# Routed token rows kept as two 16-bit planes and fetched transposed by the DMA queue

## What is computed

```python
x = layernorm(x + attention(x))          # 16 heads, 4 shared key/value heads, causal
logits = einsum('ed,btd->bte', gate_w, x)
scores = sigmoid(logits) + gate_b
weights, indices = top_k(scores, 4)      # 4 of 16 experts for each token
weights = weights / weights.sum(-1)
shared = silu(x @ w1_shared) * (x @ w3_shared) @ w2_shared
# routed expert e on a token row: silu((x @ w1[e]) * (x @ w3[e])) @ w2[e]
x = layernorm(x + shared + sum of the four routed results, weighted)
```

## Time and profile before

| | |
|---|---|
| runs, median (lowest to highest) | 598.32 us (597.01 to 599.32) |
| span of the profiled execution, first to last instruction | 564.5 us |
| median less span, what lies around the instructions | 33.8 us |
| PE / PEld busy | 527.0 / 358.6 us |
| DVE / ACT / POOL busy | 439.9 / 370.1 / 295.3 us |
| DMA packets, bytes | 53693, 64.95 MB |

### The profile page before, as it was taken

How to read it: one execution, slowest core, us unless ns; L and a number is a source line. 1 busy time by engine, 2 the same in 40 slices (tenths; PEclk the granted TensorE clock), 3 DMA queues, 4 the chain that set the end, 5 groups by cost and what they waited for, 6 DMA issues and landing times.

```text
span 564.5 us, 12179 instructions
## 1 busy us (share of the span) xinstructions
PE 527.0 (93%) x3786; PEld 358.6 (64%) x3786; DVE 439.9 (78%) x1122; ACT 370.1 (66%) x831; POOL 295.3 (52%) x340
## 2 busy tenths in 40 slices
PE   8999999999999899989999898899999999999770
PEld 4656444445454454534433487799999999999760
DVE  2387989899889799999991269988787877876582
ACT  2444767787888588869688574467676767676132
POOL 5121231656304657358888773777545454544671
PEclk9999999999999899989999999999999999999995
DMA  5954174500632902321132541586444334321962
GB/s 145 173 75 54 30 196 131 82 5 20 99 89 63 211 30 60 65 77 60 42 123 80 167 131 40 166 257 204 150 142 128 117 109 131 117 82 46 398 233 74
DMA packets 53693, 64.95 MB, mean 115 GB/s; under 512 B 8075, under 2 KB 47390, under 8 KB 53632
## 3 DMA queue, kind: packets, MB, share of 16 engines
q1 hardware_dynamic: 45952, 46.45, 32.0%
q0 software_dynamic: 7056, 17.60, 9.0%
q10 hardware_dynamic: 624, 0.13, 0.1%
HBM read 32.49 MB, written 25.62 MB: 103 GB/s over the span
## 4 chain that ended last, share of the span: by engine, by line
PE 70%; DVE 13%; POOL 6%; issue 4%; ACT 2%; DMA 2%; SPq 1%; ACTq 0%; POOLq 0%; DVEq 0%
PE psH L1678 14%; PE psS L1479 10%; PE psO L1464 9%; PE psT L1449 8%; PE psS L1541 4%; POOL xs_scratch L755 3%; DVE MX L1143 3%; PE psG L1689 3%; PE psX L1646 3%; PE psS L1484 2%; PE psY L1702 2%; PE psY L1706 2%; PE psY L1703 2%; PE psY L1704 2%; PE psY L1705 2%
## 5 line engine op out<-in xcount | busy, mean ns | idle before, releaser
L882 ACT ACTIVATE prob<-psT 128x512 f32<-128x512 f32 (+3 forms) x384 | 167.6, 496 | 54.4 <-PE psT L1449 51.9
L1143 DVE TENSOR_REDUCE MX<-psS 128x1 f32<-128x512 f32 (+3 forms) x344 | 183.2, 597 | 11.4 <-PE psS L1484 5.6
L1479 PE MATMUL psS<-KS,QS 96*128 96x512 bf16 (+3 forms) x384 | 110.9, 330 | 4.9 <-DVE MX L1143 2.5
L828 POOL DMA_INDIRECT y_scratch<-ys,dst x79 | 77.1, 976 | 65.6 <-ACT ys L1037 50.7
L1449 PE MATMUL psT<-QS,KS 98*128 98x512 bf16 (+3 forms) x384 | 107.8, 330 | 1.6 <-DMA QS<-MT 0.7
L784 POOL TENSOR_SCALAR_AFFINE_SELECT prob<-prob 128x512 f32<-128x512 f32 x64 | 42.5, 665 | 97.7 <-ACT prob L882 97.5
L1464 PE MATMUL psO<-prob,V 128*32 128x512 f32 (+3 forms) x768 | 82.8, 506 | 1.1 <-POOL prob L784 1.0
L1678 PE MATMUL psH<-wU,xh 128*128 (+1 forms) x380 | 80.7, 334 | 0.5 <-DVE z L1295 0.4
L755 POOL DMA_INDIRECT xs_scratch<-x1row,slotu x64 | 65.7, 1027 | 26.9 <-issue 16.2
L1449 PEld LDWEIGHTS psT<-QS,KS 98*128 98x128 bf16 x384 | 33.9, 98 | 54.6 <-ACT prob L882 34.2
L1479 PEld LDWEIGHTS psS<-KS,QS 96*128 96x128 bf16 x384 | 37.4, 99 | 46.0 <-DVE MX L1143 23.8
(11 more groups left out here) (252 smaller groups left out, 990.3 us busy)
## 6 DMA issues: line engine op xcount, KB each, us to landing
xs<-xs_scratch SPq DMA_DIRECT2D x80, 134.0 KB, 2.3
y<-y_scratch SPq DMA_DIRECT2D x16, 512.0 KB, 10.1
QS<-qp SPq DMA_DIRECT2D x48, 128.0 KB, 5.1
wU_raw<-in_L_ffn_w_routed_dram SPq DMA_DIRECT2D x32, 176.0 KB, 3.6
xs_scratch<-padrow SPq DMA_DIRECT2D x1, 2144.0 KB
xs_scratch<-padrow SPq DMA_DIRECT2D x16, 134.0 KB
x1row<-in_L_attn_x_dram SPq DMA_DIRECT2D x4, 512.0 KB, 6.3
out_dram<-x1row SPq DMA_DIRECT2D x8, 256.0 KB, 2.2
```

What stands on the lines that cost most here:

```text
L828: nc.gpsimd.indirect_dma_start(y4_dram, bass.IndirectOffsetOnAxis(ap=dst[:, n % NSEL, t:t + 1], axis=0), ys[:, n % NYS, t, :], None, bound ...
L882: nc.scalar.activation(prob[:, step % NPROB, h, 0:HALF - c0], ps[:, 0:HALF - c0], ACT.Exp).then_inc(s_Tfree, 1)
L1143: nc.vector.tensor_reduce(out=MX[:, c0 // HALF, heads[0]:heads[-1] + 1, i - TH * q], in_=src, op=ALU.max, axis=AX_X).then_inc(s_Sfree, 1)
L1479: last = mm(ps[:, e * dist:e * dist + cols], QS[0:ROWS, QAT[(k // 2) % NSLOT], g % 2 * G + h, (i - TH * q) * P:(i - TH * q + 1) * P], KS[b ...
```

## The change

Rows of `xs_scratch` become 272 floats, used as 544 16-bit numbers: twice (256 halves of the channels, then 8 floats of expert numbers, destinations and weights). The first 256 are the low 16 bits of each channel, the second 256 the high 16 bits ("planes"). They are built in `x1p`, one buffer of four tiles: by POOL for h = 0 to 2, by ACT for the last group. As `x1p` is used by each group in turn, POOL waits before a group's first copy until all 16 scatters of the group before have landed (L775 of the new file). POOL also copies expert numbers, destinations and weights into `x1p`, six small copies a group.

The fetch of a tile is now a `dma_start_transpose` of (256 half rows) x (256 channels) 16-bit numbers, which lands as 128 partitions x 2 x 256 in `xsT`; read as float32 that is the transposed tile. A second small DMA fetches the fields into `xm`. `xsT` shares its memory with `xl`, in 4 buffers, so SP waits for the `up` of four pairs before. PE's `rows_back` does nothing for routed pairs; `xh` and `xl` are made from `xsT`. `t` is written over `h`, `r` over `x1`, and `x1L` lies elsewhere.

```diff
-META = 3 * TOPK
-ROW = C + META
+META = 8
+HALFROW = C + 2 * META
+ROW = HALFROW
-NXS, NYS, NSEL = 3, 2, 6
+NXS, NYS, NSEL = 4, 2, 6
...
+        def planes(engine, to, row):
+
+            src = row.bitcast(U16).rearrange("p (c h) -> p h c", h=2)
+            if engine is nc.scalar:
+                return engine.copy(to, src)
+            return engine.tensor_copy(to, src)
...
+                sp.wait_ge(s_up, EARLY + n - NXS + 1)
                 if n >= NXS:
-
-                    sp.wait_ge(s_xT, EARLY + n - NXS + 1)
                     sp.wait_ge(s_sel, n - NXS + 1)
                 for t in range(2):
-                    sp.dma_start(xs[:, n % NXS, t, :], xs_dram[bass.ds(rows[2 * (n % 2) + t], P), :]).then_inc(s_xs[n % NXS], 16)
+                    at = bass.ds(rows[2 * (n % 2) + t], P)
+                    sp.dma_start_transpose(xsT[:, (EARLY + n) % NXS, t, :, :],
+                                           xs16[at, :].rearrange("r (h c) -> (r h) c", h=2)[:, 0:C]).then_inc(s_xs[n % NXS], 16)
+                    sp.dma_start(xm[:, n % NXS, t, :, :],
+                                 xs_dram[at, :].rearrange("r (h c) -> r h c", h=2)[:, :, P:P + META]).then_inc(s_xs[n % NXS], 16)
...
                 if n == 0:
+                    pool.wait_ge(s_const, CONSTS)
+                    if h:
+                        pool.wait_ge(s_scat[h - 1], 16 * TH * TOPK)
+                    pool.wait_ge(s_pick, h + 1)
+                    for half in range(2):
+                        nc.gpsimd.tensor_copy(x1f[:, :, half, P:P + TOPK].rearrange("p i (k a) -> p i k a", a=2),
+                                              idf[:, :, 2 * half:2 * half + 2].unsqueeze(3).to_broadcast([P, TH, 2, 2]))
...
                     pool.wait_ge(s_slot, h + 1)
...
+                    pool.wait_ge(s_meta, 2 * (h + 1))
+                if k == 0:
+                    if (b, q) != (B - 1, NHALF - 1):
+                        planes(nc.gpsimd, x1p[:, i, :, 0:C], x1[:, tile_of(b, q * TH + i), :]).then_inc(s_plane, 1)
+                    pool.wait_ge(s_plane, TH * h + i + 1)
...
+                    if item in LATE:
+
+                        act.wait_ge(s_scat[GROUPS - 2], 16 * TH * TOPK)
+                        act.wait_ge(s_x1, LN_NO[("ln", b, i)])
+                        planes(nc.scalar, x1p[:, i % TH, :, 0:C], x1[:, tile_of(b, i), :]).then_inc(s_plane, 1)
...
             def split_rows(m):
 
-                act.wait_ge(s_xT, m + 1)
+                if shared(m):
+                    act.wait_ge(s_xT, XT_NO[m])
+                    src = psX[:, :, :, :]
+                else:
+                    n = m - EARLY
+                    act.wait_ge(s_xs[n % NXS], 64 * (n // NXS + 1))
+                    src = xsf[:, m % NXS, :, :, :]
...
             def rows_back(m):
 
+                if not shared(m):
+                    return
```

More of the change, by code:

```diff
@@ L230 @@
 LASTCP = ("cp", B - 1, TT - 1)
+XT_NO = {m: n + 1 for n, m in enumerate(m for m in range(NPAIR) if m < EARLY or m >= EARLY + NRP)}
 UNDER = 5
@@ L276, in attention_moe @@
         eps_pow = sb("eps_pow", [P, TH])
-        x1row = sb("x1row", [P, NT, ROW])
+        x1 = sb("x1", [P, NT, C])
+        x1p = sb("x1p", [P, TH, 2, HALFROW], U16)
         padrow = sb("padrow", [P, ROW])
+        idf = sb("idf", [P, TH, TOPK])
+        wts = sb("wts", [P, TH, TOPK])
+        dtab = sb("dtab", [P, NT, TOPK])
         cpb_b = sb("cpb_b", [P, C])
@@ L327, in attention_moe @@
         xh = sb("xh", [P, 2, 2, KC, P], F32R)
-        xl = sb("xl", [P, 2, 2, KC, P], F32R)
+        at_xl = place[0]
+        xl = sb("xl", [P, NXS, 2, KC, P], F32R)
         h1 = sb("h1", [P, 2, HID])
         z = sb("z", [P, 2, HID])
-        t_ = sb("t", [P, 2, HID])
         w_ = sb("w", [P, 2, 2 * P])
@@ L334, in attention_moe @@
         gl = sb("gl", [P, 2, 2, 2, P], F32R)
-        x1L = sb("x1L", [P, 2, KC, P])
         work_end = place[0]
+        place[0] = at_xl
+        xsT = sb("xsT", [P, NXS, 2, KC, 2 * P], U16)
         place[0] = work
@@ L398, in attention_moe @@
         wBt = sb("wBt", [P, 3, C], F32R)
-        assert place[0] <= moe_end
-        place[0] = moe_end
-        r = sb("r", [P, 2, C])
+        place[0] = max(place[0], moe_end)
         rc = sb("rc", [P, G * TH])
@@ L448, in attention_moe @@
         s_pick = sem("s_pick")
+        s_plane = sem("s_plane")
+        s_meta = sem("s_meta")
         s_slot = sem("s_slot")
@@ L492, in attention_moe @@
         block = ctx.enter_context(nc.Block())
-        x1 = x1row[:, :, 0:C]
-        ID, WT, DT = slice(C, C + TOPK), slice(C + TOPK, C + 2 * TOPK), slice(C + 2 * TOPK, ROW)
+        x1f = x1p[:, :, :, :].rearrange("p i h c -> p (i h c)").bitcast(F32).rearrange("p (i h c) -> p i h c", i=TH, h=2)
+        xsf = xsT[:, :, :, :, :].rearrange("p n t k c -> p (n t k c)").bitcast(F32).rearrange(
+            "p (n t k c) -> p n t k c", n=NXS, t=2, k=KC)
+        xs16 = xs_dram.bitcast(U16)
         def tile_of(b, i):
@@ L752, in scatter_rows @@
                 if n == 0:
-                    pool.wait_ge(s_slot, h + 1)
-                    pool.wait_ge(s_const, CONSTS)
+                    pool.wait_ge(s_const, CONSTS)
[5 more added lines that the diff above has]
+                                              idf[:, :, 2 * half:2 * half + 2].unsqueeze(3).to_broadcast([P, TH, 2, 2]))
+                    t0 = tile_of(b, q * TH)
+                    for half in range(2):
+                        field = x1f[:, :, half, P + TOPK:P + META].rearrange("p i (k a) -> p i k a", a=2)
+                        nc.gpsimd.tensor_copy(field[:, :, :, 1], dtab[:, t0:t0 + TH, 2 * half:2 * half + 2])
+                    pool.wait_ge(s_slot, h + 1)
+                    for half in range(2):
+                        field = x1f[:, :, half, P + TOPK:P + META].rearrange("p i (k a) -> p i k a", a=2)
+                        nc.gpsimd.tensor_copy(field[:, :, :, 0], wts[:, :, 2 * half:2 * half + 2]).then_inc(s_meta, 1)
+                    pool.wait_ge(s_meta, 2 * (h + 1))
[3 more added lines that the diff above has]
+                    pool.wait_ge(s_plane, TH * h + i + 1)
                 nc.gpsimd.indirect_dma_start(
-                    xs_dram, bass.IndirectOffsetOnAxis(ap=slotu[:, h, i, k:k + 1], axis=0),
-                    x1row[:, tile_of(b, q * TH + i), :], None, bounds_check=NX * REG - 1,
+                    xs16, bass.IndirectOffsetOnAxis(ap=slotu[:, h, i, k:k + 1], axis=0),
+                    x1p[:, i, :, :].rearrange("p h c -> p (h c)"), None, bounds_check=NX * REG - 1,
                     oob_is_err=False).then_inc(s_scat[h], 16)
@@ L945, in run @@
                     act.wait_ge(s_rstd, n + 1)
-                    nc.scalar.activation(x1[:, tile_of(b, i), :], r[:, n % 2, :], ACT.Identity, scale=rs1[:, n % 3, 0:1],
+                    row = x1[:, tile_of(b, i), :]
+                    nc.scalar.activation(row, row, ACT.Identity, scale=rs1[:, n % 3, 0:1],
                                          bias=sh1[:, n % 3, 0:1]).then_inc(s_x1, 1)
@@ L1677, in up @@
                     for a, k, n in parts:
-                        last = mm(psH[:, t, 0:2 * HID], a[:, m % 2, t, k, :], wU[:, e, n, k, :],
+                        last = mm(psH[:, t, 0:2 * HID], a[:, m % (2 if a is xh else NXS), t, k, :], wU[:, e, n, k, :],
                                   start=((a, k, n) == parts[0]), stop=((a, k, n) == parts[-1]))
```

90 lines of the change are left out of this document (43 added, 47 removed).

## The result

| | before | changed |
|---|---|---|
| runs, median (lowest to highest) | 598.82 us (597.01 to 601.52) | 620.43 us (618.71 to 625.45) |
| ratio | | 1.0366, 95% interval 1.0324 to 1.0407 |
| span of the profiled execution | 564.5 us | 616.3 us (in a run of 618.71 us) |
| DMA packets, those under 512 B | 53693, 8075 | 107453, 72075 |

What follows compares the result with a forecast made beforehand. TensorE was taken to bound the steady pairs and POOL the end of attention. -4 + 11.5 + 0.5 + 1.6 + 0.3 + 0.3 = +10.2 us on the 564.5 us span, 608.5 us for the median; range 594 to 630.

Steps and rivals of the forecast that it cites:

- SP: the step that failed: Fetch of routed pairs: SP busy 1.9 us of each 3.88, no pair late, transposing DMAs at 0.600 us each.
- Rival 3: Routed pairs: the fetch becomes the bound, from 1.6 us per transposing DMA on; 630 or 665 us; chance 0.17.
- ring: Routed pairs: ACT and DVE instructions waiting on each other, 3.85 us a pair, 3.88 after the change, limiting the gain.
- 240: Routed pairs: us slower overall if the skill page's DMA transpose figure held, eight blocks a pair taking 10.5 us.
- Steady pairs, -4 us: Routed pairs: removing four transposes a pair cuts the period by 0.12 us, times 34; ends 0 and -14.6.
- POOL in attention, +11.5 us: End of attention: POOL's added copies and waits lie on the path; from +8 to +22 us.
- landing waits: POOL in attention: two waits for the previous group's scatters, 2.0 us each, 4.0 together; ends 3.2 and 8.8.
- small copies: POOL in attention: twelve copies of 8 or 16 numbers a partition, 0.15 us each, 1.8 together; ends 1.1 and 3.5.
- planes copies: POOL in attention: eight copies at 0.67 us plus 0.1 for the DMA's wait, 6.2 us; ends 4.4 and 10.
- ACT's four copies, +1.6: Behind attention: four planes copies on ACT, three ahead of work the chain waits for; from 0 to 2.5 us.
- 33.8 us between span and median: Whole kernel: this difference was taken as fixed, so the sum made against the 564.5 us span was added to the median.
- slower, 0.70: Whole kernel: chance that the change makes it slower, the forecast and the case of the fetch as bound taken together.

Runs made afterwards that it cites:

- e15: The kernel before with the routed pairs' transposes left out (rows where columns are wanted); 558.9 us, before 569.8, ratio 0.985.
- e2: The changed kernel with its transposing DMA made a plain one of the same bytes; 575.9 us, before 568.9.
- e4: The kernel before with the routed pairs' transposes left out, on another quick chip; 558.9 us, ratio 0.982 to before.
- e14: The changed kernel, unchanged, run again on a quick chip; 618.2 us, before 569.8, ratio 1.088.
- e16: The kernel before without the routed pairs' transposes, and VectorE's `product` issued ahead of `match`; 554.2 us.
- e18: The kernel before with both 12 row-tile copies and the landing waits added on POOL; 607.3 us beside 600.8, ratio 1.012.
- e11: The kernel before with 12 row-tile copies added on POOL ahead of scatters, into an unused tile; 604.5 us beside 600.5, ratio 1.010.
- e13: The kernel before, unchanged, profiled again on a quick chip; 569.8 us, span 564.3 us.
- e21: The changed kernel with each transposing DMA cut in two by rows; 714.0 us, where before takes 599.5.
- e5: The changed kernel with each transposing DMA cut in two by columns; 708.4 us, where before takes 600.5.
- e12: The kernel before with only POOL's landing wait ahead of the scatters of groups 1 to 3; 602.8 us beside 600.5, ratio 1.010.

## Why the prediction was wrong

**The parts, on the quick kind of chip:** before 569.8; transposes gone, -10.9 (e15); POOL's and ACT's additions, +17.0 (e2 against e4); the transposing fetch, +42.3 (e14 against e2); together 618.2. By the spans of the profiles these are -8.7, +14.7 and +43.8; each term is good to some 2 us. The three steps come from two chips of one kind, which agree within 1 us on before and on the version without transposes.

1. **SP: the step that failed.** "Taken at the 0.600 us of a 128 KB issue for the transposing ones, SP is busy for 1.9 us of 3.88, and no pair is late." A transposing DMA holds SP for 1.21 us, the fields' DMA for 0.55, and each is followed by 0.13 to 0.20 us: 4.24 us a pair with nothing else in the queue, 4.90 with pads, register loads and the few slower ones. The term stood in the sum at nothing and was worth 42 us. Without it (e2) the change costs 7.0 us on that chip, near the +10.2 forecast, in part by luck: the gain from the transposes and the cost of POOL's additions were both put too low. I had taken the price of an operation that no row shows from a plain DMA of as many bytes, and the price of the fields' DMA from the rows' fetch, though it reads twice as many pieces.
2. **Rival 3 was the case**, with its place rightly named (SP) but its threshold wrong: I had it decide from 1.6 us per transposing DMA on, and by that the measured 1.21 would have been hidden. With 0.33 for the fields and no gaps that was (3.88 - 0.66) / 2. With 0.55, four gaps of 0.17 and the true ring of 3.70 us it is (3.70 - 1.1 - 0.7) / 2 = 0.95 us, and 1.21 was over it. That should have moved the chance.
3. **The rules of the Trainium skill.** SP is held for 1.21 us by a transposing DMA and for 0.333 or 0.43 (e2) by a plain one, and this issue sets the time. The Trainium skill makes these DMAs as fast as plain ones (Advanced Engine Details and Errata, section on the X-bar transpose). For the issuing queue that does not hold here; of the transfers the runs show only that the DMA share is 0.56 with the transposing DMAs and 0.54 with plain ones. The Trainium skill's preference for TensorE (VectorE: DVE Perf Modes, section on rules for kernel authors) was right in direction. The 1309 ns for 128x128 that the Trainium skill gives (same page, section on the three transpose paths) are not what these runs show: the eight blocks of a pair pass in 4.24 us with the fields' DMAs, and the loss is 42 us and not 240 (which 6.5 us for each of 40 pairs would even make 260).
4. **Steady pairs, -4 us.** The removal is worth 9 to 11. The ring is there, but 3.70 us long and not 3.85 to 3.88: I had added `dst` with its whole 0.23 us, and in e15 the next `z` starts 0.11 us behind the start of `dst`. That is 0.12 of the 0.15 us; the wait of `xl` inside the ring hardly changed (0.54 for 0.57). The 0.03 us for `xh` from SBUF were right (617 ns in e15 for 588). PE alone needs 3.60 (e16), as the earlier trace rows had it (3.57).
5. **POOL in attention, +11.5 us.** 14.7 by the trace; e18 and e11 show the same prices with nothing else changed. The landing waits (4.0 forecast, 4.0 measured) and small copies (1.8 and 1.8) were right. The planes copies were mis-sized: 8 x 1.11 = 8.9 for 8 x 0.77 = 6.2. The copy itself was nearly right (0.61 for 0.67); the wait of the scatter for its own copy was 0.80 us, not 0.1, from which the usual 0.30 goes off.
6. **ACT's four copies, +1.6.** From the first to the seventh `z` e14 falls back by 2.0 us. That agrees, but no run has these copies alone.
7. **"I take the 33.8 us between span and median as fixed."** Wrong: 1.7 us lie around the span of e13 and 2.4 around that of the changed kernel. The other 32 were the difference between two kinds of chip. It made the forecast in microseconds a forecast for a kernel whose profile I had not seen: by the steps above the loss is 48 us on the chip of the profile, and 21.6 on the chips of the first runs, as before loses 30 us there to waits that the changed kernel hardly feels. The parts were not taken on those chips.
8. The direction (slower, 0.70) and the range (594 to 630) held; they held with rival 3's mechanism and not with the forecast's. The range held by luck too, since the base of 598.3 us was that of a slower chip; on the chip of the profile its bounds, -4 and +32 us, would have been missed by the 48 us.

## What to carry to other kernels

Before a transfer is called hidden, add up what its queue is held for: every DMA of the queue by its own kind and by its pieces, the gaps between, and the register loads and stores that share the queue, against the period. Where a kind of DMA is not in the trace, its price on the issuing queue is the largest unknown of the sum, and the threshold from which it decides should be worked out with the gaps in. A gap between the span of one execution and the median of others can be another chip, as the 6% here were, and not work around the instructions. And a ring of instructions is read from start to start: the last one's whole duration is too much where the next one starts before it ends.

## What the runs showed of the hardware

- A transposing DMA of 16-bit numbers holds the queue that issues it for 1.2 us, whether it moves 128x256, 256x128 or 256x256 of them (e21, e5, e14); a plain one of 128 rows of about 1 KB holds it for 0.33 (before) or 0.43 (e2).
- A plain DMA of 256 pieces of 32 bytes holds SP for 0.55 us, one of 128 pieces of 48 bytes for 0.42. The latter holds ACT for 0.34, and in the pair shown two of them put off ACT's next instruction by 0.65.
- A DMA issued by POOL that waits for POOL's own copy starts 0.80 us after the copy's end, one behind another such DMA 0.30 us.
- Chips differ: the kernel before takes 569 us on some and 600 on others, where the profile shows waits of up to 8.5 us (e12) that it puts down to no engine or queue of the core.
